# Attention kernel on one core: small transposes moved behind the values of their group, and zero products added between the maxima of one run

## What is computed

```python
# stage 1: attention over the 1024 points of each image, 8 heads of 8 channels
q, k, v = proj(Wq, bq), proj(Wk, bk), proj(Wv, bv)
attn = softmax(einsum('bhnd,bhmd->bhnm', q, k) * scale)
out  = einsum('bhnm,bhmd->bhnd', attn, v) @ Wo.T + bo
x    = group_norm(out) * gn_w + gn_b + x
# stage 2: four layers of attention without softmax, 8 heads each, on normed tokens
t = t + attn_layers(layer_norm(t))
# stage 3: a mixture of 8 experts, top 2, on normed tokens
t = t + experts(layer_norm(t))
```

## Time and profile before

| what | value |
|---|---|
| median of three executions (range) | 258.97 us (257.91 to 261.03) |
| the profiled execution, its own time | 261.05 us |
| its span in the trace | 259.3 us |
| TensorE busy, share of the span | 239.4 us, 92% |
| VectorE busy | 199.2 us, 77% |
| ScalarE busy | 173.2 us, 67% |
| GpSimd busy | 46.5 us, 18% |
| mean granted TensorE clock | 0.974 |

### The profile page before, as it was taken

One profiled execution on the slowest core, in us unless ns is written; L12 is line 12 of the kernel. 1 busy time (PEld: TensorE's weight loads), 2 busy tenths in 40 slices (PEclk: granted clock), 3 DMA queues, 4 the chain that ended last, 5 costly groups with the idle time before them and its releaser, 6 DMA issues.

```text
span 259.3 us, 6287 instructions
## 1 busy us (share of the span) xinstructions
PE 239.4 (92%) x2378; PEld 129.2 (50%) x2378; DVE 199.2 (77%) x432; ACT 173.2 (67%) x364; POOL 46.5 (18%) x84
## 2 busy tenths in 40 slices
PE   7999999999999999999999999999799898789994
PEld 6454355455454554455544554444334685558410
DVE  2898958998999989999899999999201584349763
ACT  2736547797887977978779788788878341329710
POOL 6964196210000100101002100010000000000340
PEclk9999957999999999999999999999899999999999
DMA  4034200152032130450300000000000000000002
GB/s 132 0 116 143 75 1 3 51 197 64 7 81 58 32 82 15 111 173 3 96 4 0 4 0 5 4 1 4 1 3 1 3 0 3 0 3 0 1 3 81
DMA packets 6102, 10.10 MB, mean 39 GB/s; under 512 B 2240, under 2 KB 3840, under 8 KB 5944
## 3 DMA queue, kind: packets, MB, share of 16 engines
q1 hardware_dynamic: 6072, 9.70, 12.6%
HBM read 6.84 MB, written 2.62 MB: 37 GB/s over the span
## 4 chain that ended last, share of the span: by engine, by line
PE 68%; ACT 13%; DVE 9%; issue 6%; DMA 1%; POOL 1%; DVEq 0%; SPq 0%; ACTq 0%; POOLq 0%
PE psum L580 23%; PE psum L519 12%; PE psum L485 11%; ACT probs L1051 9%; DVE half_max L1213 4%; PE psum L550 3%; PE psum L854 2%; PE psum L543 1%; ACT o_sb L1040 1%; PE psum L618 1%; PE psum L449 1%; PE psum L763 1%; DMA wqk_sb<-in_wqk 1%; PE psum L461 1%; PE psum L753 1%
## 5 line engine op out<-in xcount | busy, mean ns | idle before, releaser
L1213 DVE TENSOR_REDUCE half_max<-psum 128x1 f32<-128x512 f32 x256 | 158.2, 681 | 13.2 <-PE psum L485 13.0
L1051 ACT ACTIVATE probs<-psum 128x512 f32<-128x512 f32 x228 | 120.2, 604 | 30.7 <-PE psum L519 28.2
L485 PE MATMUL psum<-kop,qop 64*128 64x512 f32 x256 | 89.7, 448 | 0.8 <-DVE kop L1193 0.2
L519 PE MATMUL psum<-qop,kop 64*128 64x512 f32 x256 | 85.0, 447 | 0.1
L580 PE MATMUL psum<-probs,v_aug 128*32 128x256 f32 (+1 forms) x1296 | 76.0, 353 | 1.0 <-ACT o_sb L1040 1.0
L485 PEld LDWEIGHTS psum<-kop,qop 64*128 64x128 f32 x256 | 41.7, 189 | 20.6 <-DVE half_max L1213 12.1
L519 PEld LDWEIGHTS psum<-qop,kop 64*128 64x128 f32 x256 | 40.2, 189 | 22.7 <-ACT probs L1051 9.9
L580 PEld LDWEIGHTS psum<-probs,v_aug 128*32 128x32 f32 x1296 | 33.7, 112 | 32.0 <-issue 17.9
L939 POOL TENSOR_TENSOR attn<-o_tok,rden 128x64 f32<-128x64 f32 x15 | 4.5, 297 | 111.2 <-DVE rden L1202 103.0
L1047 ACT ACTIVATE probs<-psum 128x1024 f32<-128x1024 f32 x14 | 13.6, 1034 | 2.4 <-PE psum L519 2.3
L1202 DVE RECIPROCAL rden<-o_tok 128x8 f32<-128x8 f32 x15 | 2.9, 195 | 14.5 <-ACT o_tok L1070 14.5
(11 more groups left out here) (186 smaller groups left out, 188.5 us busy)
## 6 DMA issues: line engine op xcount, KB each, us to landing
parts_scratch<-early SPq DMA_DIRECT2D x4, 512.0 KB, 3.4
qop<-parts_scratch SPq DMA_DIRECT2D x28, 64.0 KB
vt_sb<-in_vt SPq DMA_DIRECT2D x1, 1024.0 KB, 5.2
kop<-parts_scratch SPq DMA_DIRECT2D x14, 64.0 KB
kop<-parts_scratch SPq DMA_DIRECT2D x28, 32.0 KB
x_sb<-in_x SPq DMA_DIRECT2D x2, 256.0 KB, 3.2
q_pair<-in_q_pairs SPq DMA_DIRECT2D x1, 512.0 KB, 3.9
qop<-max_row SPq DMA_DIRECT2D x28, 4.0 KB
```

Of the source, the lines that this page charges most:

```text
L485: last = nc.tensor.matmul(psum[:, m % MAX_BANKS, :], qop[at, b * PP + pp, qh * NH + t * P:qh * NH + (t + 1) * P], kop[at, b * PP + pp, c * ...
L519: last = nc.tensor.matmul(psum[:, bank, :], kop[at, b * PP + pp, mt * P:(mt + 1) * P], qop[at, b * PP + pp, qh * NH:(qh + 1) * NH], start= ...
L1051: last = nc.scalar.activation(probs[:, n % P_RING, h, :], psum[:, bank, :], ACT.Exp, scale=SCALE)
L1213: V.tensor_reduce(half_max[:, i, c, h * HT + t:h * HT + t + 1], psum[:, m % MAX_BANKS, :], AX_X, ALU.max, negate=True).then_inc(S["slot_fr ...
```

## The change

Two things are done. In `after_pair` the two steps change places: the values of the group come first, then the small jobs of that pair. It holds for all small jobs that go through `after_pair`: 13 max_t and 15 out_t, and max_r of block 1 (the max_t of the one block that falls in the wide runs is issued from the loop itself and stays). The numbering of jobs, the banks and all waits are the same. And `fill` takes a bank, a column and the start flag; between the four maxima products at the end of run 1 it is called four times, which is 32 zero products, into columns 256 to 383 of bank 7. These columns are not used by the values. With `start=False` they add zeros to what lies there and leave the accumulation of the values in that bank as it is. The older call does what it did.

```diff
-            def fill():
+            def fill(bank, at, start):
                 for _ in range(FILL):
-                    nc.tensor.matmul(psum[:, ST_BANKS[1], 0:P], idle[:, 0:P], idle[:],
-                                     start=True, stop=True, skip_group_check=True)
+                    nc.tensor.matmul(psum[:, bank, at:at + P], idle[:, 0:P], idle[:],
+                                     start=start, stop=True, skip_group_check=True)
...
             def after_pair(p):
-                small_work(p)
                 if p in values_goal:
                     values_until(values_goal[p])
+                small_work(p)
...
-                    fill()
+                    fill(ST_BANKS[1], 0, True)
...
                         for c in range(HALVES):
+                            if g:
+                                fill(PV_BANK, QB, False)
                             max_half(v, c)
```

## The result

The changed kernel takes 252.29 us in the median of four executions (251.0 to 252.56); the kernel before has 259.07 us over its four (257.91 to 261.03). The ratio is 0.972, with a 95% interval from 0.965 to 0.979: 6.8 us faster, where 252.8 us was forecast. Here and in the table of experiments a ratio leaves out executions more than 1.5% above the fastest of their kernel, which the medians hold. The profiled execution is the fastest of the four, 251.0 us with a span of 249.2 us; the profiled one of the kernel before was its slowest, at 261.05. The two profiles stand 10.05 us apart and the medians 6.8, and this difference has to be explained too.

A forecast was written before the change was run, and what follows sets the result against it. TensorE's order was taken to set the pace in the doubled runs, VectorE starving behind its waits. 261.05 - 5.7 (move) - 3.5 (clock) + 0.6 (zeros) + 0.3 (max_r) = 252.75, say 252.8 us; range 250.3 to 257.2.

The forecast's parts named there:

- What bounds the kernel: Doubled runs: TensorE's order sets the pace, its waits before small jobs starve VectorE; 7.9 us idle before reductions.
- The move: Small jobs behind the values in the doubled runs: 5.7 us gained, nine tenths of 6.3 us of waits; bounds 0 to 6.3.
- What would be late next: After the move, ScalarE's copies, VectorE's reciprocal, the row DMAs and the wide out_t were each costed at nothing.
- Max_r: Block 1's one job: ScalarE's two copies now lie ahead of the next exponential; cost 0.3 us, bounds 0 and 0.8.
- The zeros' cost: End of run 1: TensorE comes to run 2 some 1.3 us later, mostly covered; cost 0.6 us, between 0 and 1.5.
- The full clock: Behind run 1, from 31.84 to 42.04 us: zeros hold the clock, 3.5 us gained; bounds 0 and 3.95.
- A: As rival: clock falls all the same, move works, 256.6 us, chance 0.17; as piece: second to third block maximum.
- B: As rival: clock holds, wait only moves, 257.5 us, chance 0.10; as piece: third to last block maximum, steady doubled runs.
- C: As rival: maxima rows land too late, some 262 us, chance 0.03; as piece: last block maximum to ScalarE's table load.
- D: Rival: no change, the two gains at 0 with costs of 0.9, 259.9 us from the median; chance 0.04.

The follow-up runs named there:

- e1: The kernel before once more, no edit: 259.08 us in the median, ratio 1.002.
- e2: The kernel before with only the small jobs moved behind the values, no zeros in run 1: 252.82 us, ratio 0.979.
- e5: The changed kernel with only max_t behind the values, out_t and max_r in front: 253.50 us, ratio 0.983 to the kernel before.
- e6: The changed kernel with only out_t behind the values, max_t and max_r in front: 254.97 us, ratio 0.987 to the kernel before.
- e7: The changed kernel with four zeros instead of eight ahead of each maximum and max_r in front of the values: 251.08 us, ratio 0.973 to the kernel before.
- e9: The changed kernel without zeros ahead of the four maxima, but 16 ahead of the wide runs' max_t: 251.23 us, ratio 0.976 to the kernel before.
- e10: The changed kernel with two zeros ahead of each maximum and 16 ahead of the wide runs' max_t: 250.64 us, ratio 0.970 to the kernel before.
- e3: The kernel before with only the eight zeros ahead of each maximum, small jobs in front as before: 258.11 us, ratio 0.999.
- e4: The changed kernel with four zeros instead of eight ahead of each of the four maxima: 251.64 us, ratio 0.976 to the kernel before.
- e8: The changed kernel with four zeros ahead of each maximum and 16 ahead of the wide runs' max_t: 250.82 us, ratio 0.971 to the kernel before.

## Why the prediction was right, and where its terms were off

**What bounds the kernel.** Right. TensorE's order set VectorE's pace in the doubled runs; with TensorE's waits gone, VectorE's idle time fell to 1.5 us and a block went from 137.90 / 13 = 10.61 to 130.68 / 13 = 10.05 us. Forecast was 10.1.

**The move, 5.7 us forecast, at most 6.3.** It brought 7.2 us in the profile pair (B) and 6.2 in the medians of e1's group and e2, which also differ by the clock. This term was too small, by 1.5 us in the profile pair, and its upper bound was no bound. The step that failed is "what is in it: 6.3 us", the idle time printed ahead of the small jobs taken for the whole loss. In the earlier trace rows the printed wait is 0.19 us. By start times, the kernel before had 59.32 - 57.22 = 2.10 us from the last maximum to the next products (that maximum's row is below), and the changed kernel has 1.86: 0.24 us saved.

```profile
57.22 0.50 PE L485 MATMUL psum<-kop,qop 64*128 64x512 f32 x1
```

A matmul's end is modelled, 0.50 us behind its start; the values in the changed kernel start 0.44 us behind the same kind of product (53.99, 54.43). So some 0.05 us of this wait was hidden in the modelled end of the product ahead of it (0.24 against the printed 0.19; around out_t 0.32 against 0.26). The same difference of start times can be taken at all places of the doubled runs: summed over the 13 max_t it is 24.73 us before and 20.57 after, over the 13 out_t 23.11 and 19.29. That is 4.2 + 3.8 = 8.0 us, 1.7 more than was printed, and it is what e5 and e6 show one by one (4.0 and 4.0 over 13 blocks). The nine tenths that I counted, for VectorE's own pace, were right: 7.2 / 8.0 is 0.90, and by the last 12 blocks (6.5 x 13 / 12 = 7.0) it is 0.88.

**What would be late next: nothing.** Right for the score products, for the reciprocal and for the rows. The wide out_t cost nothing either: from the score products behind the first of them to ScalarE's last copy of the output it is 200.64 - 191.32 = 9.32 us before and 190.62 - 181.31 = 9.31 after. ScalarE waits for max_t at 9 jobs now, 3.5 us in all (before, 0.4 us once). No cost of it shows: its idle time before exponentials fell from 30.7 to 13.9 us on the page.

**Max_r, 0.3 us.** In the profile a wait of 0.41 us for ScalarE's rows shows up once. By e7 it costs 0.28 us in A, near the forecast, and 0.0 in A + B, because with four zeros the first max_t of B waits for GpSimd in either case. It was not ScalarE that caught up.

**The zeros' cost, 0.6 us.** TensorE came to run 2 at 33.05 instead of 31.51 us, 1.5 us late where 1.3 was forecast; the four maxima start 0.97 to 0.99 us apart (29.78 to 32.72), not 0.9. Four zeros more cost 0.84 us in A and 0.43 to 0.49 in A + B, where GpSimd takes back the rest; the forecast had 0.6 for all eight, which four alone exceed in A. What eight cost against none at a held clock could not be measured, since without zeros the clock held in no profile.

**The full clock, 3.5 us.** Right for the profiled execution as a sum: A fell by 2.5 us net, and 3.5 less the 0.6 and the 0.3 is 2.6. Term by term, 10.2 us of low clock cost 3.6 us in A against a run with four zeros; take off 0.84 for four zeros more and 0.28 for max_r, and 2.5 is left. What the first four cost is in neither term. The step that failed is not this one but its use for the median. I supposed that faster executions had lost less to the clock and would end at the same place. Mostly they had lost less, and they do end near there; but then, for the median, the sum is other: with e1 as the typical profile (258.98 us, 6.8 us of low clock, no dent) the move gives 137.71 - 130.68 = 7.0 us, A gives 12.63 - 11.49 = 1.1, and C takes 17.69 - 16.57 = 1.1 back, because the changed kernel's profile had the dent and e1's had not. That makes 7.0. The spans are 257.2 - 249.2 = 8.0 us apart; the other 0.9 lies ahead of A (32.10 against 31.17), where no edit is. Less the 1.3 us by which the changed kernel's profiled execution lies under its own median, 6.7 is left, and the medians are 6.8 apart. The forecast of 252.8 came within 0.5 us because two errors met, which is luck: counted from 261.05 the sum took off 8.3 us where the profiles show 10.05, and the profiled changed execution, at 251.0, was 1.3 us under its own median. Why the other three took 1.0 to 1.6 us longer, with mean clocks of 0.990 to 0.993, is not shown; no profile of them was taken.

**The rivals.** A (the clock falls all the same) did not happen behind run 1 in any profile with four or eight zeros. The rule of the Trainium skill weighed there, that idle gaps let the clock fall (TensorE: Matmul & The Clock Gate, "Why this matters for your kernels"), does not cover what the traces show: the clock fell with a maximum every 0.6 us, in e1, e2 and e9 alike, and in e10 with two zeros between them. B (the wait only moves) is refuted by the 0.0 us ahead of L543 and L550 and by B in e2; the 1 us by which its price of 257.5 was lowered comes from no row. C (rows late) did not occur: no wait for a DMA in the doubled runs. D needed A and B at once and falls with them.

## What to carry to other kernels

An in-order engine's small job that waits for another engine belongs behind work whose operands are surely there, at equal order of everything else; this one edit was worth 2.1% (e2's ratio). Take the loss from the start times of the instructions on both sides, not from the idle time that is printed between them. And before a low clock in one profile is priced, look at the mean clock of every execution: what an execution as fast as the median loses was here about half of it (1.4 of 3.0 us in A + B). A gain in one place can also be stopped at the next engine that no edit touched, as here by GpSimd's `MEMSET`; a term measured as nothing may only be hidden.

## What was not expected of the hardware

The length of the low stretch behind one and the same code was 3.4, 6.8, 10.2 and 13.6 us in four profiles without zeros, and it cost 1.0, 1.4, 3.0 and 4.8 us in A + B (each against the run with four zeros and the same order of the small jobs, for jobs in front against e3, less the 0.46 of its four more zeros). Per microsecond at 1.2 GHz that is 0.2 to 0.35 us. The runs compared with have the wait of 0.4 to 0.6 us for GpSimd, which takes back part. In A alone the four cost 1.4, 2.2, 3.6 and 5.1 us (with 0.84 in place of the 0.46), 0.32 to 0.41 us per microsecond. That is still less than the half that TensorE's own work would lose at half the clock; VectorE's lead and its own pace would explain it, which no run separates. Products on nothing but zeros held the clock: with eight or four of them ahead of each maximum it was at 1.00 behind run 1 in every profile. Not every execution was profiled: with four zeros, 4 of 18 (e4, e7, e8) had a mean clock of 0.980 to 0.985, and with eight, 3 of 30 (all in e3 and e6) had 0.967 or 0.984; where theirs was low is not shown.
